# Two products of an attention step exchanged in TensorE's queue

## The reference, cut to what matters

```
q = (layernorm(x) @ Wq + bq)      # 512 queries, 16 heads of 32
k = (ctx @ Wk + bk)               # 8192 keys from ctx (8192 x 384)
v = (ctx @ Wv + bv)
scores = einsum(q, k) / sqrt(32)
attn = softmax(scores, axis=-1)
out = einsum(attn, v)             # then two dense layers, residual
```

## Time and profile before

| | |
|---|---|
| median of 3 runs | 3832.69 us (3829.67 to 3832.87) |
| profiled execution, its own time | 3828.8 us |
| its span | 3827.0 us |
| mean granted TensorE clock | 0.931 of full speed |
| TensorE matmul busy | 3378.3 us, 88% |
| VectorE busy | 2385.9 us, 62% |
| ScalarE busy | 1569.4 us, 41% |
| GpSimd busy | 2048.4 us, 54% |

### The profile page before, as it was taken

How to read it: one execution, slowest core, us unless ns; L and a number is a source line. 1 busy time by engine, 2 the same in 40 slices (tenths; PEclk the granted TensorE clock), 3 DMA queues, 4 the chain that set the end, 5 groups by cost and what they waited for, 6 DMA issues and landing times. The chain is left out here.

```text
span 3827.0 us, 43808 instructions
## 1 busy us (share of the span) xinstructions
PE 3378.3 (88%) x16760; PEld 2011.5 (53%) x16760; DVE 2385.9 (62%) x3622; ACT 1569.4 (41%) x2813; POOL 2048.4 (54%) x534
## 2 busy tenths in 40 slices
PE   5999999999999876569869999999999998755697
PEld 3566666666666332124635666666666663321246
DVE  3666666666666346983536666666666663479745
ACT  1455555555555413210104555555555554132101
POOL 1577777777777702510015777777777777025100
PEclk8899999999999887789879999999999999877899
DMA  4212122222121022031142121222221210220310
GB/s 119 53 41 61 40 62 53 49 51 63 38 67 34 18 94 100 0 111 45 43 132 51 43 58 40 62 53 48 51 63 38 67 34 18 94 100 0 111 68 32
DMA packets 89840, 220.45 MB, mean 58 GB/s; under 512 B 23264, under 2 KB 25312, under 8 KB 84832
## 3 DMA queue, kind: packets, MB, share of 16 engines
q1 hardware_dynamic: 89632, 217.65, 20.6%
HBM read 107.35 MB, written 2.23 MB: 29 GB/s over the span
## 5 line engine op out<-in xcount | busy, mean ns | idle before, releaser
L709 DVE TENSOR_REDUCE pm<-ps 128x1 f32<-128x512 f32 x2048 | 1395.5, 690 | 835.0 <-PE ps L1167 815.9
L1008 ACT ACTIVATE pf<-ps 128x512 f32<-128x512 f32 x2048 | 1200.8, 600 | 1101.7 <-PE ps L1193 1101.7
L582 POOL TENSOR_TENSOR psum<-psum,pf 128x2048 f32<-128x2048 f32 x256 | 1168.6, 4565 | 20.1
L1167 PE MATMUL ps<-ks,qs 96*128 96x512 f32 x2048 | 1066.4, 522 | 51.8 <-POOL ks L559 31.6
L582 POOL TENSOR_TENSOR psum<-pf 128x2048 f32<-128x2048 f32 x128 | 585.1, 4571 | 623.0 <-ACT pf L1008 623.0
L1193 PE MATMUL ps<-qs,ks 98*128 98x512 f32 x2048 | 815.8, 402 | 2.9 <-ACT pf L1008 2.9
L1167 PEld LDWEIGHTS ps<-ks,qs 96*128 96x128 f32 x2048 | 394.8, 193 | 330.2 <-issue 111.4
L1203 PE MATMUL ps<-pf,V 128*32 128x512 f32 x4096 | 549.0, 608 | 1.4 <-ACT pf L1008 1.4
L1152 PEld LDWEIGHTS ps<-Wv,cT 128*128 128x128 f32 x3072 | 446.9, 191 | 154.2 <-issue 100.6
L1145 PE MATMUL ps<-cT,Wk 128*128 128x256 f32 x1536 | 471.4, 390 | 3.3 <-DVE QL L694 3.3
L1152 PE MATMUL ps<-Wv,cT 128*128 128x128 f32 x3072 | 472.1, 278 | 0.0
(11 more groups left out here) (171 smaller groups left out, 2616.7 us busy)
## 6 DMA issues: line engine op xcount, KB each, us to landing
ks<-KH SPq DMA_DIRECT2D x512, 128.0 KB, 2.3
ks<-KL SPq DMA_DIRECT2D x256, 128.0 KB, 2.3
cT<-in_ctxT SPq DMA_DIRECT2D x32, 768.0 KB, 4.5
BC<-bc_rows SPq DMA_DIRECT2D x16, 1024.0 KB, 11.5
xw<-in_W SPq DMA_DIRECT2D x4, 2048.0 KB, 10.5
wA<-in_ffn_w SPq DMA_DIRECT2D x2, 4096.0 KB, 14.7
wB<-in_ffn_w SPq DMA_DIRECT2D x2, 4096.0 KB, 25.1
wA<-in_W_fcT SPq DMA_DIRECT2D x8, 1024.0 KB, 8.1
```

The lines of the kernel that those rows point to most:

```text
L582: pool.tensor_tensor(acc, before, pf[:, tile % P_SLOTS, :], ALU.add).then_inc(s_sum, 1)
L709: dve.tensor_reduce(pm[:, n // BLK, n % BLK:n % BLK + 1], src, AX.X, ALU.max).then_inc(s_wfree, 1)
L1008: act.activation(pf[:, tile % P_SLOTS, j * NTOK:(j + 1) * NTOK], ps[:, S_BANK + u % S_BANKS, :], ACT.Exp, scale=SCALE).then_inc(s_exp, 1)
L1167: last = pe.matmul(dst, qs[0:3 * HD, h, t * P:(t + 1) * P], ks[0:3 * HD, h, i * 512:(i + 1) * 512], start=True, stop=True)
```

## The change

In each step that still has a score product, the score product of the step is issued to TensorE's queue ahead of the maximum product of the same step. Nothing else is changed: what comes after the two in the step (M, T or D, the burst, the sums, the piece of side work), the waits of each product, the banks and the queues of the other engines stay as they are.

```
@@ -1238,10 +1238,10 @@
                 fill_side(*LEAD_PIECES)
                 for i in range(STEPS):
                     if i + SB_AHEAD < UNITS:
+                        scores(i + SB_AHEAD)
                         for x in work_at(i):
                             if x[0] == "A":
                                 fill(x)
-                        scores(i + SB_AHEAD)
                     for x in work_at(i):
                         if x[0] != "A":
                             fill(x)
```

## The result

The changed kernel is slightly slower or the same. Its median is 3834.77 us (20 runs, 3830.41 to 3842.73) against 3829.64 us of the kernel before (20 runs, 3824.22 to 3835.75): ratio 1.0015, 95% interval 1.0008 to 1.0022. Run again in a later session it had 3830.56 us against 3830.53 us: ratio 0.9999, interval 0.9989 to 1.0009. The two measurements together are worth about +0.1%, 4 us, by my estimate. Both are under the 0.2% that the prediction took as the limit of a measurement, though the interval of the first leaves 1 out. The traces say more than the times, since the same distances come back in them to 0.01 us. The profiled execution has a span of 3833.0 us, against 3827.0.

A forecast was written before the change was run, and what follows sets the result against it. TensorE's own stream of work, almost without holes, was taken as the bound. Terms +4.4 (T), +3.0 (M) and -1.0 (stretch without side work) sum to +6.4, rounded to +6: median about 3838.5 us, range 3829 to 3851.

The forecast's parts named there:

- The exchange itself: Score and maximum product swapped on TensorE: the pair's length unchanged, only where each ends moves by 0.24 us; worth 0.
- T costs 0.10 us: Behind the pair, T's weight load waits for a reduction ending 0.24 us later: 0.10 us each, 4.4 us in all.
- M costs 0.05 us: Behind the pair, M's weight load is released later by VectorE's reductions: 0.05 us in each of 60 places, 3.0 us.
- The key chain: Low keys, their 12 DMAs and the waiting maximum product all 0.24 us later: 0; 16 waits swallow T's 0.10 us.
- Rival 3: Key chain not delayed, so the score product fills part of the 16 key waits: -5 to -10 us; chance 0.10.
- The stretch without side work: Last 23 steps with a maximum product per example: score goes ahead of the wait, 1 us off, between 0 and 4.2.
- Rival 1: At T and M the two waits cost nothing, weight loads being unable to start earlier anyway: -1 to +2 us; chance 0.16.
- Rival 2: Step after two without side work: the maximum product's load is released too late, 120 times 0.11, +13 us; chance 0.14.
- Rival 4: Burst right behind the pair starts at another distance: up to 0.10 us in 360 places, 36 us either way; chance 0.04.
- A wait of S for ScalarE: Sign in TensorE's stream that the prediction is wrong: the score product waiting for ScalarE, a wait taken as worth 0.

The follow-up runs named there:

- experiment 5: The changed kernel with the old order (maximum product first) in steps 11, 12, 21, 22 and 23 of every 32; ratio 1.0003 to the kernel before.
- experiment 8: The kernel before, with VectorE making the low keys ahead of T's addition and D moved from step 13 to 15, run a second time; ratio 0.9980.
- experiment 6: The change applied to the kernel before with low keys made first and D in step 15; ratio 1.0029 to the kernel before.
- Experiment 1: The changed kernel with the maximum product first again in steps 11 and 23 of every 32; ratio 1.0030 to the kernel before.
- experiment 9: The change, except in step 14, applied to the kernel before with low keys made first and D in step 15; ratio 1.0047 to the kernel before.

## Why the prediction was right

The forecast was 3838.5 us, 0.15% over the 3832.7 us then known, and no measurable change; the ratio is 1.0015 in one measurement and 0.9999 in the other. In us the measured 3834.8 lies in the range, 3.7 us under the forecast; 3.1 us of that are the kernel before, whose median over 20 runs is 3829.6. The mechanism at T and M is shown; the sum came out partly by luck, since the repetition has next to no cost where the forecast had 6 us.

- *The exchange itself costs nothing:* right. The page's rows swap their means, and experiment 5, with 27 of 32 steps exchanged, is at 1.0003.
- *T costs 0.10 us:* right. Product to T 0.280 instead of 0.234 us, T to burst 0.586 instead of 0.531 us as means of 58; 6.0 us for 60. The row of the single T that waited in the kernel before had the exact price, 0.59.
- *M costs 0.05 us:* too high. Its load is short, and the measured cost is 0.03 us (0.265 instead of 0.237 us, and 0.003 us to the burst): 1.9 us where I took 3.0.
- *The key chain costs nothing and swallows T's 0.10 us in 16 groups, 1.6 us:* mis-sized, and the argument for it was wrong. The waits in the view fell from 8.6 and 11.4 us to 3.7 and 1.0 us, and fewer groups wait, against my own sign. Not all of this is time won, since the score fills the same hole. Between the T's (58 groups) the changed kernel takes 5.5 us more in the first pair of traces and 1.4 us more in the second, where T and M alone would make 7.7: the late keys cost 2 to 6 us less, where I had 1.6. From score to score over steps 20 to 22 (without the first two groups and the last of each example) a group has 4.04 and 4.05 us before and 4.01 and 3.94 us after, beside 3.92 in the old order and 3.91 in the new with the keys early (experiments 8 and 6). Rival 3 was thus partly at work beside my forecast.

  What was wrong in the argument can be read from the traces. I argued that product and keys both shift by 0.24 us. Counted from the burst behind T, over 56 groups, the first key DMA is issued at 1.54 us instead of 1.49, and the last one has landed at 11.29 and 11.23 us on the mean instead of 11.22 and 11.21. The product of step 21 starts at 11.90 us where nothing holds it, instead of 11.57. So the keys are 0.05 us later (0.15 us with T's own 0.10 us, not 0.24) and the product 0.33 us, by the score that stands between the burst and it. How late the keys land still varies from trace to trace by as much as the gain.
- *The stretch without side work gains 1 us:* wrong, nothing. From burst to burst a plain four steps take 3.54 us in both orders. The maximum product now stands directly ahead of the burst, after a wait, and the burst follows at 0.43 us instead of 0.33. This exposed load is the step that I left out. The four steps with T take 4.38 us instead of 4.15, and the last four with an A 3.59 instead of 3.70: together 0.1 us an example to the worse.
- *Rival 1, the waits are hidden:* out. Every T and M load beside a maximum product shows its wait. So the rule of the Trainium skill ("TensorE: Matmul & The Clock Gate", "The mechanism"), that a load overlaps a matmul in flight only when their row groups differ, does not hold here as it stands: T's load ran under a score product over 98 rows in the kernel before (165.27, the score from 165.24 to 165.63). The same section opens with a second case, a load into the background weight buffer, and with that case it is not against the rows.
- *Rival 2, the step behind a pair:* out, but not by the 0.01 us that I had counted. The load comes at 834.58, 0.06 us after the first of three reductions (833.83 + 0.69), so it is just in time, and ends at 834.77, 0.05 us after the product has started at 834.72. I had taken that the load must be over before the product starts, and the rows show that it need not be: the product stands 0.319 us behind the score in this step as in a plain one (step 19, both as means of 58). Experiment 1 shows what a later release costs in this same step: 0.20 us a place.
- *Rival 4, another distance from A to the burst:* out. It is 0.33 us from either product, by the means 0.329 and 0.325.
- *A wait of S for ScalarE would show me wrong:* there is one, 0.2 us, in the second trace of the changed kernel, and one of 0.2 us in the second trace of the kernel before as well, so it is not of the change. There is none for the maximum rows.

Summed with what was measured: 6.0 (T) + 1.9 (M) less 2 to 6 (keys) is +2 to +6 us. The spans differ by +6.0 us in the first pair of traces and +0.4 us in the second (3830.2 against 3829.8), the part of it between the T's by 5.5 and 1.4 us. The sum of my terms, 6.4, was at the high end because M was too dear and the gain at the keys too small.

## What to carry to other kernels

When the bound engine's stream has no holes, exchanging two neighbours costs nothing in itself; look instead for the items that are released just in time. A weight load that starts 0.05 us after its releaser, hidden under the product ahead of it, has next to no margin left, and no wait in the profile shows it. Count the banks of a shared rotation in order, position by position, and redo it for every item that an experiment moves forward or back: three of the ten runs here (experiments 1, 6 and 9) came out slower than expected because an item met the bank of another one that I had not followed. A delay at one place also has to be followed to each of its users: here the keys moved by 0.15 us and the product that waits for them by 0.43, and the difference came back as time. And to speed such a kernel up, start the DMA chain of the one real wait earlier: that was worth 0.14 to 0.20%.

## What was not expected

- The waits for stacked keys vary with the run: 3.7 and 1.0 us in two traces of one kernel, 8.6 and 11.4 us in two of another, with an unchanged order of instructions in each. This is about the size of the whole effect under study, so a difference of 0.1% in this kernel says little without the distances in the trace.
- An exposed weight load costs the stream less than its own length: about 0.11 us of 0.19 ahead of a product of 512 columns, 0.06 of 0.14 for T's first, and 0.003 us of 0.09 for M.
- The release of a bank by VectorE shows up on TensorE 0.05 to 0.06 us after the end of the reduction, for every T and M beside a maximum product in every kernel of this study.
